# Graph kernel, aggregation stage: addresses of the accumulator computed for a group at once, and one of eight one-hot tiles made by the Vector engine

## The chip, the cores and the metric

The kernel runs on one core of one Trainium2 chip. The metric is the device time of one execution in microseconds (us). The kernel before takes 6959.23 us, the median of three runs (6958.45 to 6972.85).

## The reference

Two graph layers over 12,500 nodes with 256 features and 200,000 edges sorted by destination, each followed by a residual and a layer norm. The first layer is attention with 4 heads of 64 features:

```
scores = einsum('ehd,ehd->eh', Q[dst], K[src] + 0.2*rel[:, None, :]) / 8
w   = softmax of scores over the edges of one destination
agg = segment_sum(w[:, :, None] * V[src], dst)          # the aggregation
out = where(deg > 0, agg, V).reshape(N, 256) @ Wo + bo  # then layer norms
```

The second layer gates `leaky(x @ W2 + b2)[col]` with a sigmoid and sums it by `row`. The change touches only the aggregation of the first layer: the sum over edges of weight times value, and of the weights themselves, by destination.

## The kernel before, in words

The program runs in stages that are divided by barriers: projections and a sort, the tables of steps, the scores of the edges, the softmax's numerators, the aggregation (`aggregate`, the function of the change), the update of the nodes, the second layer (`attend`) and the last norm.

The sums live in `node_tab` in SBUF: 98 blocks of 128 nodes, each block 260 columns wide (`AW`: 256 sums of values, 4 sums of weights). The edges are cut into steps. A step is a tile of 128 edges with one block of nodes; a tile that reaches over two blocks is two steps. There are 1664 steps, taken in 416 groups of `U` = 4. The block of each step is not known when the program is built. It is read at run time from a table, `places0`, into registers of the engine.

For every group g, five engines work:

- SP starts the load of the four tiles' values from HBM into `terms` (ring of `DEEP` = 10), as soon as TensorE is through with group g - 10.
- GpSimd (POOL) multiplies the values by the weights, in place (line 1032, one instruction per group).
- ScalarE (ACT) makes the one-hot matrices. `measure(g)` takes four instructions (line 1041), one per tile: |local - iota|, where `local0` holds the edge's node within its block and `iota` the numbers 0 to 127. `encode(g)` is one instruction over the four (line 1054): relu(1 - far), which is 1 where the distance is 0. `hot` is a ring of four, and `encode(g)` waits until TensorE is through with group g - 4. `put_weights(g)` (line 1047) copies the weights beside the values.
- TensorE (PE) multiplies, per step, `hot` (128 edges by 128 nodes) with `terms` (128 edges by 260 columns) into one bank of PSUM (line 1084). An fp32 product runs as two matmuls, so there are eight per group. `ps_sum` has two buffers of four banks. TensorE waits (lines 1080 to 1083) for `hot_ready`, `weights_put`, `weighed`, and for the four additions of group g - 2.
- The Vector engine (DVE) adds each of the four results onto its block of `node_tab` (line 1072). Successive steps can have the same block, so each addition waits on the semaphore `added` until the one in front of it is complete.

The order on each engine is that of the program text. On DVE, group g is: one load of four block numbers into registers (`blocks_of`, line 150), the wait for `summed`, and then four times the wait for `added`, the computation of the address from the block number (block * 260 and so on, in the engine's registers), and the addition. The address is computed where the addition is put into the program, thus behind the wait for `added` (and, for the first of a group, behind both waits).

Of the kernel before, what the change touches and what calls it, by code (L numbers as in the profile page):

```python
# [7 lines left out]
ALU = mybir.AluOpType  # L8
ACT = mybir.ActivationFunctionType
AX = mybir.AxisListType  # L10

P = 128
# [9 lines left out]
U = 4  # L22
# [12 lines left out]
G = -(-(T + NB - 1) // TURN) * V  # L35
# [4 lines left out]
AW = D + H  # L40
# [105 lines left out]
def blocks_of(nc, eng, places, g):  # L146


    at = (g % QUARTER) * U
    return nc.values_load_multi_w_load_instructions(  # L150
        places[g // QUARTER * 32:g // QUARTER * 32 + 1, at:at + U], engines=[eng.engine], min_val=0, max_val=NB - 1,
        skip_runtime_bounds_check_because="the merged order of tiles and blocks ends at the last block")[1]
# [11 lines left out]
def gnn_kernel(nc, x, src, dst, edge_type, query, wq, bq, wk, bk, wv, bv, rel_w, wo, bo, gamma, beta,  # L164
               w1, b1, w2, b2, wa1, ba1, wa2, ba2, out):
    with ExitStack() as ctx:
# [24 lines left out]
        with ExitStack() as layer0:  # L191
            t["other0"] = layer0.enter_context(nc.sbuf_tensor("other0", [P, S], i32))
            t["places0"] = layer0.enter_context(nc.sbuf_tensor("places0", [P, S // 4], i32))
            t["score"] = layer0.enter_context(nc.sbuf_tensor("score", [P, S * H], fp32))
            t["keys"] = [layer0.enter_context(nc.sbuf_tensor(f"keys{u}", [P, F], i32)) for u in range(2)]
            t["two_signs"] = layer0.enter_context(nc.sbuf_tensor("two_signs", [P, 8], fp32))
            t["local0"] = t["keys"][0][:, 0:S].bitcast(fp32)
            project(nc, t, query, wq, bq, wk, bk, wv, bv)
            build_steps(nc, t, 0)
            edge_scores(nc, t, rel_w)  # L200
            softmax_numerators(nc, t)
            aggregate(nc, t)
# [796 lines left out]
def aggregate(nc, t):  # L999
    with ExitStack() as ctx:  # L1000
        def sb(name, shape, dt=fp32):
            return ctx.enter_context(nc.sbuf_tensor(name, shape, dt))

        def sem(name):
            return ctx.enter_context(nc.semaphore(name))

        tab = t["node_tab"]
        hot = [sb(f"a_hot{u}", [P, U, P]) for u in range(4)]
        far = [sb(f"a_far{u}", [P, U, P], bf16) for u in range(3)]
        terms = [sb(f"a_terms{u}", [P, U, AW]) for u in range(DEEP)]  # L1010
        ps_sum = [ctx.enter_context(nc.psum_tensor(f"ps_sum{u}", [P, U, 512], fp32)) for u in range(2)]
        rows_in, weights_put, weighed = [sem(f"a_rows_in{u}") for u in range(DEEP)], sem("a_weights_put"), sem("a_weighed")
        far_ready, hot_ready, summed, added = sem("a_far_ready"), sem("a_hot_ready"), sem("a_summed"), sem("a_added")
        block = ctx.enter_context(nc.Block())

        @block.sync
        def _(sp):
            for g in range(G):
                if g >= DEEP:
                    sp.wait_ge(summed, g - DEEP + 1)  # L1020
                sp.dma_start(terms[g % DEEP][:, :, 0:D],
                             t["v_edges"][g * U * P:(g + 1) * U * P, :].rearrange("(k p) d -> p k d", p=P)).then_inc(rows_in[g % DEEP], 16)

        @block.gpsimd
        def _(pool):
            for spent in t["spent"]:
                pool.sem_clear(spent)
            for g in range(G):
                pool.wait_ge(rows_in[g % DEEP], 16 * (g // DEEP + 1))
                weight = t["score"][:, g * U * H:(g + 1) * U * H].rearrange("p (k h) -> p k h", h=H)  # L1030
                by_head = terms[g % DEEP][:, :, 0:D].rearrange("p k (h d) -> p k h d", h=H)
                nc.gpsimd.tensor_tensor(by_head, by_head, weight.unsqueeze(3).broadcast_to([P, U, H, DH]), ALU.mult).then_inc(weighed, 1)  # L1032

        @block.scalar
        def _(act):
            def measure(g):
                if g >= 3:
                    act.wait_ge(hot_ready, g - 2)
                for k in range(U):
                    at = g * U + k  # L1040
                    last = nc.scalar.activation(far[g % 3][:, k, :], t["iota"][:, :], ACT.Abs, scale=-1.0, bias=t["local0"][:, at:at + 1])  # L1041
                last.then_inc(far_ready, 1)

            def put_weights(g):
                if g >= DEEP:
                    act.wait_ge(summed, g - DEEP + 1)
                nc.scalar.copy(terms[g % DEEP][:, :, D:AW],
                               t["score"][:, g * U * H:(g + 1) * U * H].rearrange("p (k h) -> p k h", h=H)).then_inc(weights_put, 1)

            def encode(g):  # L1050
                if g >= 4:
                    act.wait_ge(summed, g - 3)
                act.wait_ge(far_ready, g + 1)
                nc.scalar.activation(hot[g % 4][:, :, :], far[g % 3][:, :, :], ACT.Relu, scale=-1.0, bias=t["ones"][:, 0:1]).then_inc(hot_ready, 1)  # L1054

            measure(0)
            for g in range(G):
                if g + 1 < G:
                    measure(g + 1)
                encode(g)  # L1060
                put_weights(g)

        @block.vector
        def _(dve):
            for g in range(G):
                blocks = blocks_of(nc, dve, t["places0"], g)
                dve.wait_ge(summed, g + 1)
                for k in range(U):
                    acc = tab[:, bass.ds(blocks[k] * AW, AW)]
                    if g * U + k:  # L1070
                        dve.wait_ge(added, g * U + k)
                    dve.tensor_tensor(acc, acc, ps_sum[g % 2][:, k, 0:AW], ALU.add).then_inc(added, 1)  # L1072
            dve.wait_ge(added, G * U)

        @block.tensor
        def _(pe):
            for g in range(G):
                pe.wait_ge(hot_ready, g + 1)
                pe.wait_ge(weights_put, g + 1)
                pe.wait_ge(weighed, g + 1)  # L1080
                if g >= 2:
                    pe.wait_ge(added, (g - 1) * U)
                for k in range(U):
                    last = nc.tensor.matmul(ps_sum[g % 2][:, k, 0:AW], hot[g % 4][:, k, :], terms[g % DEEP][:, k, :],  # L1084
                                            start=True, stop=True)
                last.then_inc(summed, 1)
# [540 lines left out]
```

## Time and profile before

| | |
|---|---|
| median of three runs | 6959.23 us |
| the profiled execution's own time | 6949.19 us |
| its span, first to last instruction | 6947.4 us |
| aggregation, first to last addition starts | 3152.3 to 4136.2 us |
| mean TensorE clock over the whole span / in the aggregation | 0.77 / 1.00 |
| share of the span: PE, DVE, POOL, ACT busy | 65%, 64%, 62%, 40% |

"L1072" is line 1072 of the program. PE is TensorE's matmuls, PEld its weight loads, which run beside them. "Idle before" is the time an engine did no work ahead of the named instructions, with what it was waiting for. Instructions that an engine's sequencer handles by itself (reading a table into registers, computing an address, waiting) are not counted as busy; the profile gives them the engine's name with a q, as DVEq. Starts are in us from the start of the span.

### The profile page before, as it was taken

How to read it: one execution, taken by the hardware profiler on the slowest of the kernel's cores; microseconds unless marked ns; L12 is line 12 of the kernel's file. 1: busy time of each engine (PE TensorE's matmuls, PEld its weight loads, DVE VectorE, ACT ScalarE, POOL GpSimd, SP SyncE). 2: the span in 40 equal slices, each digit the busy share in tenths (PEclk: the TensorE clock that was granted, in tenths of full speed). 3: DMA queues.
4: the chain of work that ended last, by engine and by line, in shares of the span. 5: the costliest groups of instructions: out<-in, count | busy, mean ns of one | idle time of the engine just before them, and what ended most of it. 6: DMA issues, size and time to landing. Idle time of an engine off the chain costs nothing. (4 is left out here: it accounts for less than half of the span.)

```text
span 6947.4 us, 76698 instructions
## 1 busy us (share of the span) xinstructions
PE 4539.0 (65%) x16367; PEld 3185.0 (46%) x16367; DVE 4423.0 (64%) x9005; ACT 2772.4 (40%) x6174; POOL 4284.4 (62%) x4006
## 2 busy tenths in 40 slices
PE   9766776667667565637888879965555555555553
PEld 5555555555555444425666654433333333333331
DVE  8766776767767555576777778954444444444447
ACT  2233333333333333328888866732222222222223
POOL 0066766767767655518788755556666666666662
PEclk9867677776777677769999999976676777676766
DMA  4388998989899888826777653345555555555554
GB/s 147 118 283 292 292 294 295 294 290 298 290 299 293 292 281 275 278 66 218 223 223 222 223 160 100 103 120 140 141 143 139 141 142 139 142 142 140 142 140 133
DMA packets 920948, 1405.60 MB, mean 202 GB/s; under 512 B 92203, under 2 KB 697635, under 8 KB 920185
## 3 DMA queue, kind: packets, MB, share of 16 engines
q0 software_dynamic: 208288, 644.62, 30.0%
q1 hardware_dynamic: 645305, 640.62, 29.3%
q10 hardware_dynamic: 66914, 115.46, 5.5%
q8 instruction: 158, 2.59, 0.2%
q14 instruction: 283, 2.32, 0.1%
HBM read 1127.23 MB, written 273.11 MB: 202 GB/s over the span
## 5 line engine op out<-in xcount | busy, mean ns | idle before, releaser
L676 POOL DMA_INDIRECT s_rows<-kv_rows,other x1664 | 1749.5, 1051 | 893.4 <-issue 488.6
L1434 POOL DMA_INDIRECT t_rows<-xj_rows,other x1564 | 1492.6, 954 | 781.8 <-issue 443.1
L1526 PE MATMUL ps_xsum<-t_rows,t_att 128*128 x3328 | 1208.6, 523 | 1060.4 <-DVE t_att L1487 644.0
L1526 PEld LDWEIGHTS ps_xsum<-t_rows,t_att 128*128 128x128 f32 x3328 | 807.0, 261 | 1462.3 <-issue 1326.4
L1466 ACT ACTIVATE t_att<-t_att,t_rows 128x128 f32<-128x128 f32 x1664 | 562.4, 392 | 1689.0 <-issue 1177.4
L1487 DVE SCALAR_TENSOR_TENSOR t_att<-iota,local,t_att 128x128 f32<-128x128 f32 x1664 | 579.0, 348 | 978.8 <-ACT t_att L1466 491.7
L787 PE MATMUL ps_q<-node_tab,hot 128*128 x3328 | 1154.0, 503 | 45.0 <-issue 44.1
L785 PE MATMUL ps_rel<-rel,hot 64*128 64x64 f32 x3328 | 590.9, 332 | 853.0 <-DVE s_rows L768 587.0
L765 DVE TENSOR_TENSOR s_rows<-s_rows,ps_rel 128x1024 f32<-128x1024 f32 x416 | 506.2, 1217 | 886.8 <-remote 699.4
L785 PEld LDWEIGHTS ps_rel<-rel,hot 64*128 64x128 f32 x3328 | 531.9, 240 | 1045.1 <-issue 902.3
L692 ACT ACTIVATE hot<-apart,ones 128x1024 f32<-128x1024 bf16 x416 | 477.7, 1148 | 1241.6 <-remote 756.9
L1084 PE MATMUL ps_sum<-a_terms,a_hot 128*128 128x260 f32 x3328 | 829.8, 392 | 169.4 <-DVE node_tab L1072 155.3
L1032 POOL TENSOR_TENSOR a_terms<-a_terms,score 128x1024 f32<-128x1024 f32 x416 | 787.1, 1904 | 193.4 <-DMA a_terms<-v_edges 180.0
L787 PEld LDWEIGHTS ps_q<-node_tab,hot 128*128 128x128 f32 x3328 | 789.2, 249 | 225.6 <-issue 59.3
L1072 DVE TENSOR_TENSOR node_tab<-node_tab,ps_sum 128x260 f32 x1664 | 706.9, 425 | 289.9 <-DVE node_tab L1072 102.3
L1495 DVE TENSOR_TENSOR node_tab<-node_tab,ps_xsum 128x256 f32 x1664 | 698.0, 419 | 212.3 <-issue 166.0
L1084 PEld LDWEIGHTS ps_sum<-a_terms,a_hot 128*128 128x128 f32 x3328 | 599.1, 190 | 400.1 <-issue 326.7
L687 ACT ACTIVATE apart<-apart,minus_p 128x1024 bf16<-128x1024 bf16 x416 | 473.8, 1139 | 409.5 <-DMA apart<-what_rows 275.5
L1041 ACT ACTIVATE a_far<-iota,keys 128x128 bf16<-128x128 f32 x1664 | 530.0, 389 | 4.7 <-PEq L807 4.7
L768 DVE TENSOR_TENSOR s_rows<-s_rows,ps_q 128x1024 f32<-128x1024 f32 x416 | 507.7, 1220 | 14.3
L770 DVE TENSOR_REDUCE score<-s_rows 128x16 f32<-128x1024 f32 x416 | 507.4, 1220 | 14.2
L1054 ACT ACTIVATE a_hot<-a_far,ones 128x512 f32<-128x512 bf16 x416 | 300.3, 722 | 154.8 <-PE ps_sum L1084 154.8
(218 smaller groups left out, 3559.4 us busy)
## 6 DMA issues: line engine op xcount, KB each, us to landing
v_edges<-s_rows SPq DMA_DIRECT2D x416, 512.0 KB
a_terms<-v_edges SPq DMA_DIRECT2D x416, 512.0 KB, 4.4
apart<-what_rows SPq DMA_DIRECT2D x416, 256.0 KB
t_att<-a_rows ACTq DMA_DIRECT2D x416, 256.0 KB
s_rows<-kv_rows,other POOLq DMA_INDIRECT x1664
t_rows<-xj_rows,other POOLq DMA_INDIRECT x1564
kv_rows<-kv_out SPq DMA_DIRECT2D x97, 256.0 KB, 2.0
xj_rows<-n_hx SPq DMA_DIRECT2D x97, 130.0 KB, 2.4
```

Of the source, the lines that this page charges most:

```text
L676: pool.indirect_dma_start(out=rows[g % KV_RING][:, k, :], out_offset=None, in_=t["kv_rows"], in_offset=bass.IndirectOffsetOnAxis(ap=t["oth ...
L785: nc.tensor.matmul(ps_rel[g % 2][:, k, :], hot[g % 2][0:R, 1, k, :], rel_02[:, :], start=True, stop=True)
L787: last = nc.tensor.matmul(ps_q[g % 2][:, k, :], hot[g % 2][:, 0, k, :], t["node_tab"][:, bass.ds(blocks[k] * AW, D)], start=True, stop=True)
L1032: nc.gpsimd.tensor_tensor(by_head, by_head, weight.unsqueeze(3).broadcast_to([P, U, H, DH]), ALU.mult).then_inc(weighed, 1)
L1041: last = nc.scalar.activation(far[g % 3][:, k, :], t["iota"][:, :], ACT.Abs, scale=-1.0, bias=t["local0"][:, at:at + 1])
L1072: dve.tensor_tensor(acc, acc, ps_sum[g % 2][:, k, 0:AW], ALU.add).then_inc(added, 1)
L1084: last = nc.tensor.matmul(ps_sum[g % 2][:, k, 0:AW], hot[g % 4][:, k, :], terms[g % DEEP][:, k, :], start=True, stop=True)
L1434: pool.indirect_dma_start(out=rows[:, at:at + XW], out_offset=None, in_=t["xj_rows"], in_offset=bass.IndirectOffsetOnAxis(ap=t["other1"][: ...
L1466: last = nc.scalar.activation(att[g % ATT_RING][:, k, :], att[g % ATT_RING][:, k, :], ACT.Sigmoid, bias=rows[:, bass.ds(slot[k] * XW + D, 1)])
L1487: dve.scalar_tensor_tensor(w, t["iota"][:, :], t["local1"][:, g * U + k:g * U + k + 1], w, ALU.is_equal, ALU.mult)\
L1495: dve.tensor_tensor(acc, acc, ps_sum[g % 4][:, k, :], ALU.add).then_inc(added, 1)
L1526: nc.tensor.matmul(ps_sum[g % 4][:, k, :], att[g % ATT_RING][:, k, :], rows[:, bass.ds(slot[k] * XW, D)], start=True, stop=True)\
```

## The change

ScalarE leaves out the fourth tile's one-hot in every odd group (`by_act`). DVE makes it: `encode_last(g)` is one comparison, `iota == local`, with `iota` read from a copy of the numbers in the unused columns 384 to 511 of the last bank of `ps_sum[1]`. It writes into the same place in `hot`. It is issued behind the first addition of an odd group, for the group four later; groups 1 and 3 get theirs ahead of the loop. TensorE waits for one more semaphore, `last_hot`, in odd groups.

`sums_of(g)` reads the four block numbers and calls `lower_ap` on the four accumulators, which computes their addresses at that place in the program. It is issued between the second and the third addition of group g - 1. Ahead of the first addition, the wait for `added` now comes before that for `summed`.

```diff
+        ps_iota = ps_sum[1][:, U - 1, 512 - P:512]
+        def by_act(g):
+            return U - g % 2
...
-                for k in range(U):
+                for k in range(by_act(g)):
                     last = nc.scalar.activation(far[g % 3][:, k, :], ...)
...
-                nc.scalar.activation(hot[g % 4][:, :, :], far[g % 3][:, :, :], ACT.Relu, ...)
+                nc.scalar.activation(hot[g % 4][:, 0:by_act(g), :], far[g % 3][:, 0:by_act(g), :], ACT.Relu, ...)
...
         def _(dve):
+            def sums_of(g):
+                sums = [tab[:, bass.ds(block * AW, AW)] for block in blocks_of(nc, dve, t["places0"], g)]
+                for acc in sums:
+                    dve.lower_ap(acc)
+                return sums
+
+            def encode_last(g):
+                at = g * U + U - 1
+                if g >= 4:
+                    dve.wait_ge(summed, g - 3)
+                dve.tensor_scalar(hot[g % 4][:, U - 1, :], ps_iota, t["local0"][:, at:at + 1], None, ALU.is_equal).then_inc(last_hot, 1)
+
+            dve.tensor_copy(ps_iota, t["iota"][:, :]).then_inc(iota_put, 1)
+            dve.wait_ge(iota_put, 1)
+            encode_last(1)
+            encode_last(3)
+            sums = sums_of(0)
             for g in range(G):
-                blocks = blocks_of(nc, dve, t["places0"], g)
-                dve.wait_ge(summed, g + 1)
-                for k in range(U):
-                    acc = tab[:, bass.ds(blocks[k] * AW, AW)]
+                for k, acc in enumerate(sums):
                     if g * U + k:
                         dve.wait_ge(added, g * U + k)
+                    if k == 0:
+                        dve.wait_ge(summed, g + 1)
                     dve.tensor_tensor(acc, acc, ps_sum[g % 2][:, k, 0:AW], ALU.add).then_inc(added, 1)
+                    if k == 0 and g % 2 and g + 4 < G:
+                        encode_last(g + 4)
+                    if k == 1 and g + 1 < G:
+                        following = sums_of(g + 1)
+                sums = following
...
         def _(pe):
                 pe.wait_ge(hot_ready, g + 1)
+                if g % 2:
+                    pe.wait_ge(last_hot, max(g // 2 + 1, 2))
```

## Rows read from the trace of the kernel before

**Rows 1.** Busy time by stretch, a piece of the aggregation; (x) is instructions.

```profile
core 0: us, PE busy (x) PEld busy (x) DVE busy (x) ACT busy (x) POOL busy (x), PEclk, DMA share, GB/s
3360.00:3560.00 200.00, 168.40 (x678) 121.62 (x678) 143.51 (x338) 168.99 (x508) 160.63 (x85) 1.00 0.70 223
```

**Rows 2.** Waits, 3200 to 4100 us: total, times, longest.

```profile
POOL a_terms L1032 <- DMA a_terms<-v_edges: 176.6, 264, 1.9
PE ps_sum L1084 <- DVE node_tab L1072: 142.4, 381, 0.7
ACT a_hot L1054 <- PE ps_sum L1084: 140.9, 381, 0.7
DVE node_tab L1072 <- DVE node_tab L1072: 93.1, 398, 0.6
```

**Rows 3.** Timeline of DVE, single additions: start us, duration us; two group starts, one step.

```profile
3603.55 0.42 DVE L1072 TENSOR_TENSOR node_tab<-node_tab,ps_sum 128x260 f32 x1
3604.18 0.42 DVE L1072 TENSOR_TENSOR node_tab<-node_tab,ps_sum 128x260 f32 x1 [0.21 <-DVE node_tab L1072]
3604.75 0.42 DVE L1072 TENSOR_TENSOR node_tab<-node_tab,ps_sum 128x260 f32 x1
...
3606.52 0.43 DVE L1072 TENSOR_TENSOR node_tab<-node_tab,ps_sum 128x260 f32 x1 [0.21 <-DVE node_tab L1072]
```

**Rows 4.** Single lines: duration ns min/median/max, first and last start us.

```profile
L1072 DVEq FUSED_REGOPS  x1664: 57/57/65, 3152.2 to 4136.1; - x185
L1072 DVE TENSOR_TENSOR node_tab<-node_tab,ps_sum x1664: 424/424/427, 3152.3 to 4136.2; 128x260 f32 x185
...
L150 DVEq TENSOR_LOAD <-places x2: 340/342/344, 3603.6 to 3605.9; - x2
...
L1461 ACTq FUSED_REGOPS  x416: 13/152/1393, 4598.2 to 6849.7; - x139
...
L1080 PEldq EVENT_SEMAPHORE  x416: 51/51/51, 3148.6 to 4129.4; - x139
```

**Rows 5.** Timeline of DVE in the scores' stage: dependent instructions without addresses.

```profile
745.15 1.21 DVE L765 TENSOR_TENSOR s_rows<-s_rows,ps_rel 128x1024 f32<-128x1024 f32 x1
746.39 1.22 DVE L768 TENSOR_TENSOR s_rows<-s_rows,ps_q 128x1024 f32<-128x1024 f32 x1
747.65 1.22 DVE L770 TENSOR_REDUCE score<-s_rows 128x16 f32<-128x1024 f32 x1
```

**Rows 6.** Timeline of DVE in the second layer: addition and comparison alternate.

```profile
5500.68 0.42 DVE L1495 TENSOR_TENSOR node_tab<-node_tab,ps_xsum 128x256 f32 x1
5501.02 0.35 DVE L1487 SCALAR_TENSOR_TENSOR t_att<-iota,local,t_att 128x128 f32<-128x128 f32 x1
5501.31 0.42 DVE L1495 TENSOR_TENSOR node_tab<-node_tab,ps_xsum 128x256 f32 x1
```

**Rows 7.** Two lines of DVE with a column operand: duration ns min/median/max.

```profile
L1487 DVE SCALAR_TENSOR_TENSOR t_att<-iota,local,t_att x1664: 336/347/420, 4601.6 to 6858.5; 128x128 f32<-128x128 f32 x185
...
L545 DVE TENSOR_SCALAR hit<-ps_tile,partition x4: 1949/1950/1951, 308.9 to 4152.4; 128x1664 f32<-128x1664 f32 x4
```

**Rows 8.** Timeline of PE and ACT over one group.

```profile
3604.12 0.46 PE L1084 MATMUL ps_sum<-a_terms,a_hot 128*128 128x260 f32 x1 [0.35 <-DVE node_tab L1072]
...
3605.73 0.38 PE L1084 MATMUL ps_sum<-a_terms,a_hot 128*128 128x260 f32 x1
...
3606.15 0.72 ACT L1054 ACTIVATE a_hot<-a_far,ones 128x512 f32<-128x512 bf16 x1 [0.34 <-PE ps_sum L1084]
```

**Rows 9.** Timeline of POOL: three multiplications in a row.

```profile
3602.01 5.63 POOL L1032 TENSOR_TENSOR a_terms<-a_terms,score 128x1024 f32<-128x1024 f32 x3 [1.17 <-DMA a_terms<-v_edges]
```

More of the change, by code:

```diff
@@ L1013, in aggregate @@
         far_ready, hot_ready, summed, added = sem("a_far_ready"), sem("a_hot_ready"), sem("a_summed"), sem("a_added")
+        iota_put, last_hot = sem("a_iota_put"), sem("a_last_hot")
+        ps_iota = ps_sum[1][:, U - 1, 512 - P:512]
+        def by_act(g):
+            return U - g % 2
         block = ctx.enter_context(nc.Block())
@@ L1053, in encode @@
                 act.wait_ge(far_ready, g + 1)
-                nc.scalar.activation(hot[g % 4][:, :, :], far[g % 3][:, :, :], ACT.Relu, scale=-1.0, bias=t["ones"][:, 0:1]).then_inc(hot_ready, 1)
+                nc.scalar.activation(hot[g % 4][:, 0:by_act(g), :], far[g % 3][:, 0:by_act(g), :], ACT.Relu, scale=-1.0, bias=t["ones"][:, 0:1]).then_inc(hot_ready, 1)
             measure(0)
```

## The prediction

> **What bounds the kernel now.** I read the profile in this order: busy time by stretch, waits, the timeline of single additions, and then single lines for durations. The change touches one stage. Barriers stand on both sides of it, so whatever it gains or loses there reaches the end unchanged.
>
> In the aggregation no engine is full: of 200 us, PE is busy for 168, ACT for 169, POOL for 161 and DVE, the least, for 144, with TensorE's clock at 1.00, which is its 2.4 GHz level, and the DMA engines at 0.70 [rows 1]. The waits say who is late. PE waits for DVE's additions in nearly every group, ACT's one-hot waits for PE, and DVE waits only for itself [rows 2]. POOL waits for its loads, which come when PE frees a buffer; it runs ahead. So DVE ends last in each turn, through idle time that its busy share hides.
>
> The timeline shows this time. An addition takes 0.424 us, the next starts 0.57 after it started, and from the fourth to the next group's first it is 0.63; from group to group it is 3606.52 - 3604.18 = 2.34 us [rows 3]. Over the whole stage it is (4136.2 - 3152.3) / 415.75 = 2.366 [rows 4]; the difference, some 12 us in all, are single longer groups, and I leave it as it is. Thus 0.14 us stands between two additions. Where one DVE instruction waits for another and computes no address, only 0.03 stands there (746.39 - 745.15 - 1.21) [rows 5]. The address costs DVE about 0.11: the register instruction itself takes 0.057 [rows 4], and about 0.05 passes until what is behind it starts.
>
> **The change, part by part.** Starts of additions, from one to the next:
>
> First to second, and third to fourth: the address goes. 0.424 + 0.034 = 0.46 each, 0.11 less than now.
>
> Fourth to the next group's first: one of its two waits still stands ahead of the addition, the address doesn't. 0.63 - 0.11 = 0.53 (0.52 to 0.56).
>
> Second to third: here the sequencer reads the block numbers and computes four addresses before it can issue the third addition. The load starts as its addition does (an addition at 3603.55, the load at 3603.6) and takes 0.342 [rows 3, 4]; with about 0.025 ahead and 0.05 behind it, the addresses start at 0.42, when the addition is nearly done (0.424 + 0.034). What comes now is exposed, and no row shows it. If the four are four instructions, each 0.11 as now, the third addition starts at 0.42 + 0.43 = 0.85. If nothing of them shows, it is 0.46. The row's name says that register operations are packed, and another such row, of other content, takes 152 ns where this one takes 57 [rows 4], so one instruction can hold more than one address; the four stand side by side in the changed program, which they never do now. I take two instructions of two addresses, some 0.075 + 0.05 each: 0.42 + 0.25 = 0.67. That costs 0.10 more than now.
>
> An even group is then 0.46 + 0.67 + 0.46 + 0.53 = 2.12 us.
>
> The one-hot on DVE, in odd groups, goes between the first and second addition. Its wait is for the sum that the first addition has just used, so it is over. Its duration: a comparison of 128 columns with a column operand takes 347 ns out of SBUF, and out of PSUM 1664 columns take 1950, which is 1.04 ns a column plus 217, so 350 ns for 128 [rows 7]; both ways agree. Part of it is hidden: behind an addition that nothing makes it wait for, a comparison starts 0.34 after the addition's start, 0.08 before its end, and the next addition starts 0.29 later with an address in its way [rows 6]. Without one, 0.35 - 0.08 = 0.27: first to second is 0.61 in place of 0.46, an odd group 2.27. Bounds: 0.46 (wholly hidden) and 0.424 + 0.35 + 0.03 = 0.80 (nothing overlaps). I take 0.61, by the nearest row. What waits behind it is the second addition, and through it PE two groups on.
>
> DVE's pair of groups is 4.39 us against 2 x 2.338 = 4.68 now.
>
> What ACT is spared (one of four 0.39 us instructions and a quarter of 0.72 every second group) is worth nothing: ACT waits for PE in every group [rows 2]. POOL needs 5.63 / 3 = 1.88 a group [rows 9] and the DMA share rises to 0.70 x 2.36 / 2.2 = 0.75; both stay below. DVE's copy of the numbers, its two first one-hots and the first addresses run while POOL's first product is made: nothing.
>
> **Next in line is PE with its two buffers.** From the end of group g's last addition (3603.97) to PE's first matmul are 0.15, to the start of the last 1.61 and to its end 0.38 more, and 0.04 until ACT starts on it [rows 3, 8]: 2.18. Then come DVE's four additions of group g + 2, which take 0.46 + 0.67 + 0.46 + 0.42 = 2.01 in an even group and 2.16 in an odd one. So two groups can't go by in less than 4.19, or 4.34 by way of the odd ones. There PE has one wait more, of 0.05 [rows 4] or somewhat above: 4.40. That is level with DVE's 4.39, so the pair is 4.40. It also means that whatever goes better on DVE by 0.1 gains only a part.
>
> Sum: 208 pairs x (4.68 - 4.40) = 57 us (with 4.676: 57.4). 6949.2 - 57.4 = 6891.8 for the profiled execution. The median of the runs stands 10.0 us above that execution, so the predicted time is 6902 us.
>
> A price from a page, outside this sum: the Trainium skill, page "VectorE: DVE Perf Modes", section on the TRN2 errata, gives 120 cycles plus the columns at 0.96 GHz for PSUM to SBUF, by which I estimate the one-hot at 0.26 us. The row of 1950 ns for 1664 columns [rows 7] would be 1.86 us by it; the row disagrees, I think because of the column operand. By the page the sum would be the first rival's.
>
> **Rivals.**
>
> The one-hot costs DVE 0.09 less: first to second is 0.52 in odd groups. DVE's pair is then 4.30 and PE's way 4.31: 208 x 0.09 = 19 us more gain, 6883. Against it speaks the row of the comparison out of PSUM, which I trust (0.06).
>
> The addresses are not packed, and the load and they hold back the third addition (this ends slower). Second to third is 0.85 or, if each takes 0.12, 0.91. DVE's pair is 4.39 + 2 x (0.85 - 0.67) = 4.75, or 4.87: 15 to 40 us slower, 6974 to 6999. It decides from 0.81 upward, where 4.39 + 2 x 0.14 = 4.67 is today's pair. For it: today's addresses are one instruction each. Against: now something always stands between them (0.14, of which 0.04 for an end within 0.2%).
>
> The addresses are not kept: the addition computes its own again, and the early ones fall away. Intervals stay 0.57 and 0.63, and the one-hot adds 0.61 - 0.57 = 0.04 per pair, since it lies in the gap: 8 us, 6967. For it: in this trace no addition uses an address made ahead of another instruction. Against: an addition both reads and writes its block, and has one address row for both, so one value already serves twice (0.09).
>
> Something outside, such as a lower clock in a later stage or contention at a port by the comparisons, which eats 15 us or more of slower time: 0.03.
>
> **How the numbers follow.** The forecast holds 0.68. Its own range: second to third at 0.53 makes PE's way 4.26 and the gain 86 us, 6873; at 0.75 DVE's pair is 4.55 and the gain 26 us, 6933; thus 6870 to 6935. For 8 in 10 the range goes from 6868 to 6968, which takes in the unkept addresses and leaves out most of the unpacked ones. This kernel's time can be told from no change only beyond 0.2%, 14 us. Faster: 0.68 + 0.06 = 0.74. Within: 0.09 + 0.04 of the unpacked = 0.13. Slower: the other 0.10 of the unpacked + 0.03 = 0.13.
>
> **What would show it.** In the trace after: starts of additions 0.46, 0.67, 0.46 and 0.53 apart, with 0.61 first in odd groups; fewer address rows than 1664, each longer than 57 ns, none between a wait and its addition; a comparison of about 350 ns x208; PE still waiting for DVE, but DVE at times for PE; group to group 2.2 us. The forecast is wrong if second to third is over 0.81, if the address rows stay at 1664 with 57 ns, or if DVE now waits for PE in every group with PE's eight matmuls taking much over 2 us.

## The result, and the profile after

The changed kernel takes 6853.34 us (median of four runs, 6845.10 to 6861.07) against 6958.84 us for the kernel before, run beside it. The ratio is 0.985, 95% interval 0.9836 to 0.9864: 105 us faster. The prediction was 6902 us with a range from 6868 to 6968. The direction was right, and the gain was nearly twice what was forecast. On another chip the same pair of kernels gave 6871.64 against 6953.67 us, 0.988 (0.9862 to 0.9899).

The span went from 6947.4 to 6843.3 us, 104.1 less. The part from the first to the last addition of the aggregation took 983.9 us and takes 887.1: 96.8 less. Of the rest, 8.7 us went ahead of the stage, where the program is the same in both (the stage's first load starts at 3140.36 and at 3131.61), 0.2 came back before the first addition and 1.2 after the last. One execution differs from another by as much: the four of the changed kernel lie 16 us apart. So 97 us is what the traces show for the change. On the other chip the same part of the changed kernel took 886.8 us.

The same stretch as in [rows 1], of the changed kernel:

```profile
core 0: us, PE busy (x) PEld busy (x) DVE busy (x) ACT busy (x) POOL busy (x), PEclk, DMA share, GB/s
3360.00:3560.00 200.00, 186.97 (x752) 134.83 (x752) 167.41 (x423) 168.49 (x517) 176.98 (x94) 1.00 0.79 247
```

94 groups pass in 200 us where 85 did. ACT is as busy as before, though it has a share less to do per group, since it has more groups. The clock stayed at 1.00.

The waits, which answer to [rows 2]:

```profile
ACT a_hot L1060 <- PE ps_sum L1113: 121.3, 284, 1.0
POOL a_terms L1038 <- DMA a_terms<-v_edges: 89.2, 168, 2.5
DVE node_tab L1094 <- DVE node_tab L1094: 47.7, 192, 0.6
PE ps_sum L1113 <- DVE node_tab L1094: 43.3, 191, 0.6
DVE node_tab L1094 <- PE ps_sum L1113: 36.8, 179, 0.6
```

The last row is new in this stretch. DVE now waits for PE, and PE still waits for DVE: neither is ahead. That is the look of a loop between two engines, not of one that is full. The list leaves out idle time under 0.15 us and so counts only every second group. By starts and ends in the trace it is nearly every one: from group 10 on, PE's first matmul starts 0.15 us after the end of DVE's last addition of two groups before in all of them (0.146 to 0.148), and DVE's first addition starts 0.11 us after PE's end in 96% of them. Before the change the second time was 0.41: PE had long been done.

Single lines of DVE's program: the address rows, the one-hot, the additions (duration ns min/median/max, first and last start):

```profile
L1074 DVEq FUSED_REGOPS  x832: 93/93/104, 3132.6 to 4028.3; - x167
...
L1081 DVE TENSOR_SCALAR a_hot<-ps_sum,keys x208: 343/345/352, 3132.0 to 4021.4; 128x128 f32<-128x128 f32 x104
...
L1094 DVE TENSOR_TENSOR node_tab<-node_tab,ps_sum x1664: 412/425/427, 3143.8 to 4030.9; 128x260 f32 x185
```

832 address rows, two a group, of 93 ns each, stand in the place of 1664 of 57 ns [rows 4]. The one-hot takes 345 ns.

The timeline of DVE over an odd group, from its first addition to the next group's, with the one-hot in it, after the last two additions of the even group in front. It answers to [rows 3]:

```profile
3601.65 0.43 DVE L1094 TENSOR_TENSOR node_tab<-node_tab,ps_sum 128x260 f32 x1 [0.23 <-DVE node_tab L1094]
3602.11 0.42 DVE L1094 TENSOR_TENSOR node_tab<-node_tab,ps_sum 128x260 f32 x1
3602.74 0.42 DVE L1094 TENSOR_TENSOR node_tab<-node_tab,ps_sum 128x260 f32 x1 [0.20 <-PE ps_sum L1113]
3603.08 0.34 DVE L1081 TENSOR_SCALAR a_hot<-ps_sum,keys 128x128 f32<-128x128 f32 x1
3603.34 0.42 DVE L1094 TENSOR_TENSOR node_tab<-node_tab,ps_sum 128x260 f32 x1
3603.85 0.43 DVE L1094 TENSOR_TENSOR node_tab<-node_tab,ps_sum 128x260 f32 x1
3604.31 0.42 DVE L1094 TENSOR_TENSOR node_tab<-node_tab,ps_sum 128x260 f32 x1
3604.78 0.42 DVE L1094 TENSOR_TENSOR node_tab<-node_tab,ps_sum 128x260 f32 x1
```

First to second is 0.60, where 0.61 was forecast. Second to third is 0.51, and 0.67 was forecast. The reading of the block numbers tells why: it starts at 3603.2, ahead of the second addition, which starts at 3603.34. In the even group behind it the order is the other way round: the second addition starts at 3605.24, the reading at 3605.3:

```profile
L150 DVEq TENSOR_LOAD <-places x1: 340/340/340, 3603.2 to 3603.2; - x1
...
L150 DVEq TENSOR_LOAD <-places x1: 344/344/344, 3605.3 to 3605.3; - x1
```

```profile
3605.24 0.42 DVE L1094 TENSOR_TENSOR node_tab<-node_tab,ps_sum 128x260 f32 x1
```

Over the whole stage the reading starts 0.47 us after the group's first addition started (0.471 to 0.477), in even and in odd groups alike. The second addition starts 0.46 after the first in even groups and 0.60 in odd ones. So the reading starts 0.014 behind the second addition in the median even group, and 0.131 ahead of it in the median odd one.

The two sides of the loop. PE after DVE's last addition of the odd group, which ends at 3604.74:

```profile
3604.88 0.46 PE L1113 MATMUL ps_sum<-a_terms,a_hot 128*128 128x260 f32 x1 [0.21 <-DVE node_tab L1094]
```

And what follows PE's end of the group in front. PE's last two matmuls take from 3602.03 to 3602.63. ACT starts 0.04 after that, and DVE's addition, at 3602.74, 0.11 after it:

```profile
3602.03 0.60 PE L1113 MATMUL ps_sum<-a_terms,a_hot 128*128 128x260 f32 x2
```

```profile
3602.67 0.61 ACT L1060 ACTIVATE a_hot<-a_far,ones 128x384 f32<-128x384 bf16 x1 [0.21 <-PE ps_sum L1113]
```

### The profile page after: what moved, and what is told of

It reads as the page before. It is cut to its first block and busy times, and to the rows that moved or that the text cites. A ratio compares the mean times of both kernels' runs of the same rounds, so it can differ in the third digit from the quotient of the medians.

```text
span 6843.3 us, 75868 instructions
## 1 busy us (share of the span) xinstructions
PE 4518.4 (66%) x16367; PEld 3172.1 (46%) x16367; DVE 4457.0 (65%) x9214; ACT 2689.4 (39%) x5966; POOL 4272.2 (62%) x4006
## 5 line engine op out<-in xcount | busy, mean ns | idle before, releaser
L1038 POOL TENSOR_TENSOR a_terms<-a_terms,score 128x1024 f32<-128x1024 f32 x416 | 783.0, 1902 | 104.3 <-DMA a_terms<-v_edges 90.9
L1047 ACT ACTIVATE a_far<-iota,keys 128x128 bf16<-128x128 f32 x1456 | 469.3, 389 | 5.4 <-PEq L807 5.4
L1060 ACT ACTIVATE a_hot<-a_far,ones 128x512 f32<-128x512 bf16 (+1 forms) x416 | 278.1, 668 | 142.8 <-PE ps_sum L1113 139.3
```

## The experiments

Eleven kernels ran in three batches, each batch on one chip with the kernel before beside it. The chips differ (the kernel before took 7043.22, 6997.68 and 6953.67 us in them), so the ratios to it are what compares. The pair of groups is worked out from each trace: first to last start of an addition, divided by the 207.875 pairs between them. This mean takes in single longer groups; where a forecast left them out, the text gives the median pair beside it. The kernel before was profiled on the first chip only; the changed kernel's stage took 887.1 us there and 886.8 on another chip, so lengths of the stage can be compared across chips to some tenths of a us as far as this one pair shows.

| kernel | ratio to before (95%) | first to last addition, us | pair, us |
|---|---|---|---|
| before | 1 | 983.9 | 4.73 |
| changed | 0.985 (0.9836 to 0.9864) | 887.1 | 4.27 |
| addresses only | 0.9854 (0.9837 to 0.9870) | 882.7 | 4.25 |
| one-hot only | 1.0001 (0.9991 to 1.0011) | 986.2 | 4.74 |
| load behind fourth addition | 0.9875 (0.9858 to 0.9892) | 905.8 | 4.36 |
| release by pairs | 0.9802 (0.9785 to 0.9819) | 849.4 | 4.09 |
| loads spread, no one-hot | 0.9803 (0.9791 to 0.9816) | 842.1 | 4.05 |
| loads spread, release by pairs | 0.9723 (0.9710 to 0.9735) | 779.9 | 3.75 |
| the same with DVE's one-hot | 0.9735 (0.9722 to 0.9747) | 793.3 | 3.82 |
| waits swapped back | 0.9853 (0.9840 to 0.9865) | 879.6 | 4.23 |
| one-hot behind third | 0.9911 (0.9894 to 0.9927) | 914.6 | 4.40 |
| numbers in SBUF | 1.0042 (1.0029 to 1.0056) | 1004.8 | 4.83 |
| changed, on the last three's chip | 0.988 (0.9862 to 0.9899) | 886.8 | 4.27 |

The "last three" are the kernels one-hot behind third, numbers in SBUF, and the changed one again; they shared a chip. For the changed one 0.985 and a pair of 4.24 were expected there; its ratio is 0.988, its median pair 4.24.

### Which half did it

Addresses only:

```diff
-            return U - g % 2
+            return U
...
-            dve.tensor_copy(ps_iota, t["iota"][:, :]).then_inc(iota_put, 1)
-            dve.wait_ge(iota_put, 1)
-            encode_last(1)
-            encode_last(3)
...
-                    if k == 0 and g % 2 and g + 4 < G:
-                        encode_last(g + 4)
...
-                if g % 2:
-                    pe.wait_ge(last_hot, max(g // 2 + 1, 2))
```

> Only the addresses a group ahead; ScalarE makes all four one-hots again, DVE none. Theory A (the changed kernel's turn is set by the loop between PE and DVE over two PSUM buffers, 4.24 us a pair of groups, and the one-hot on DVE is hidden): the four additions still take 1.99 us from first start to last end, so the pair stays at 4.24, and the time at the changed kernel's, 6853 us, within 10 us; ratio to before 0.985. Theory B (taking work from ScalarE brought a part of the gain): ScalarE's one-hots come late, PE waits for them, and a good part of the 105 us is lost: 6880 us or more.

Ratio 0.9854, pair 4.25 (median 4.24): theory A, and theory B falls. The stage is 4.4 us shorter than the changed kernel's. The median pairs differ by 0.003, which is under 1 us; the rest lies in single longer groups, of which this kernel has fewer. One-hot only:

```diff
             def sums_of(g):
-                sums = [tab[:, bass.ds(block * AW, AW)] for block in blocks_of(nc, dve, t["places0"], g)]
-                for acc in sums:
-                    dve.lower_ap(acc)
-                return sums
+                return blocks_of(nc, dve, t["places0"], g)
...
-            sums = sums_of(0)
             for g in range(G):
-                for k, acc in enumerate(sums):
+                blocks = sums_of(g)
+                dve.wait_ge(summed, g + 1)
+                for k in range(U):
+                    acc = tab[:, bass.ds(blocks[k] * AW, AW)]
                     if g * U + k:
                         dve.wait_ge(added, g * U + k)
-                    if k == 0:
-                        dve.wait_ge(summed, g + 1)
...
-                    if k == 1 and g + 1 < G:
-                        following = sums_of(g + 1)
-                sums = following
```

> Only the one-hot by DVE in odd groups; block numbers and addresses as before the change, address behind the wait. Theory A: first to second addition is 0.61 in odd groups against 0.57, nothing else changes: 208 x 0.04 = 8 us slower than before, 6967 us. Theory B: 40 us or more faster than before, 6920 us or less.

Ratio 1.0001. The stage grew by 2.3 us, not 8: in odd groups first to second went from 0.569 to 0.603, as forecast, and second to third came down from 0.567 to 0.557, which was not; the median pair grew by 0.02 to 4.70. Both halves together say that the whole gain is the addresses', and the one-hot's move is worth nothing here. Theory B falls.

### What sets the time now

Release by pairs:

```diff
-                if g >= 2:
-                    pe.wait_ge(added, (g - 1) * U)
                 for k in range(U):
+                    if g >= 2 and k % 2 == 0:
+                        pe.wait_ge(added, (g - 2) * U + k + 2)
```

> The changed kernel, but PE waits for the first two additions of group g-2 before its first two products and for the other two before the rest, in place of for all four. Theory A: the loop opens by about 0.9 us, DVE's own chain of 4.05 us a pair sets the time: 208 x 0.19 = 40 us faster than the changed kernel, 6813 us, and DVE's starts are 0.46, 0.65 (0.51 in odd groups), 0.46, 0.46 apart throughout. Theory C (DVE's chain already sets it): no change, 6853 us.

Pair 4.09, and the ratio fell by 0.005, some 34 us of 6900; the stage is 37.7 us shorter. Not a single instruction of DVE was changed, and yet its turn is shorter: with four additions awaited, the loop set the time. Theory C falls. Its timeline, from an even group's third addition to the next even group's first:

```profile
3600.22 0.42 DVE L1094 TENSOR_TENSOR node_tab<-node_tab,ps_sum 128x260 f32 x1 [0.23 <-DVE node_tab L1094]
...
3601.14 0.43 DVE L1094 TENSOR_TENSOR node_tab<-node_tab,ps_sum 128x260 f32 x1
3601.48 0.35 DVE L1081 TENSOR_SCALAR a_hot<-ps_sum,keys 128x128 f32<-128x128 f32 x1
3601.74 0.41 DVE L1094 TENSOR_TENSOR node_tab<-node_tab,ps_sum 128x260 f32 x1
3602.25 0.42 DVE L1094 TENSOR_TENSOR node_tab<-node_tab,ps_sum 128x260 f32 x1
3602.71 0.42 DVE L1094 TENSOR_TENSOR node_tab<-node_tab,ps_sum 128x260 f32 x1
```

Here the odd group's first addition (3601.14) follows the fourth of the even one (0.46 after the third, at 3600.68) by 0.46 as well, where 0.53 was forecast. DVE's own pair is thus (0.46 + 0.65 + 0.46 + 0.46) + (0.60 + 0.51 + 0.46 + 0.46) = 4.06 (median 4.07): the one-hot adds nothing to it.

The load behind the fourth addition:

```diff
-                    if k == 1 and g + 1 < G:
+                    if k == U - 1 and g + 1 < G:
                         following = sums_of(g + 1)
```

> Block numbers and addresses of the next group behind the fourth addition in place of behind the second. The exposed 0.19 us moves from inside the four additions, which PE's buffer waits for, to behind them. Theory A (PE-DVE loop): four additions take 1.80 us in even groups and 1.94 in odd ones, where the one-hot isn't hidden any more; DVE's own pair is 4.19 and the loop's 4.19 by way of the odd groups: 208 x 0.05 = 10 us faster than the changed kernel, 6843 us. Theory C (DVE's own chain is what sets the changed kernel's time): DVE's pair grows by 0.14, 29 us slower, 6882 us.

This went the other way than theory A said, 18.7 us longer in the stage than the changed kernel, and not as far as C. Fourth to first took 0.72, not 0.65. The row of the wait for `summed` now stands behind the load and the addresses, so its 0.07 is exposed in every group: DVE's own pair is 2.10 + 2.23 = 4.33 (median 4.33), above the loop. PE's end stands 0.39 us ahead of the first addition in even groups and 0.26 in odd ones, so DVE does not wait for it. What the theory lacked is the price of that row; the kernel with the waits swapped back looks at it by itself. This one does not tell A from C.

### How far it goes

Loads spread, no one-hot (on the kernel with addresses only):

```diff
-                for acc in sums:
-                    dve.lower_ap(acc)
...
             sums = sums_of(0)
+            for acc in sums:
+                dve.lower_ap(acc)
...
-                    if k == 1 and g + 1 < G:
+                    if k == 0 and g + 1 < G:
                         following = sums_of(g + 1)
+                    if k in (1, 2) and g + 1 < G:
+                        for acc in following[2 * k - 2:2 * k]:
+                            dve.lower_ap(acc)
```

> Addresses only (ScalarE makes all one-hots), and DVE's register work spread: the block numbers of the next group are read behind the first addition, two addresses behind the second, two behind the third. Theory A (PE-DVE loop; each piece of register work is shorter than the addition it runs beside): DVE's starts are 0.46 apart throughout, its own pair 3.66; the four additions take 1.80 us and the loop between PE and DVE 0.15 + 1.99 + 0.11 + 1.80 = 4.04 to 4.05 a pair, against 4.24 of the changed kernel: the stage 40 us shorter than with addresses only, ratio to before 0.980. Theory D (register work is never hidden wholly, since the sequencer issues in order): the pair stays above 4.15, ratio 0.983 or more.

All additions of a group start 0.46 apart, pair 4.05, ratio 0.9803: theory A to the hundredth. Theory D falls: register work is hidden wholly in this kernel, where each piece is shorter than the addition beside it.

With the release by pairs added to that:

> As the kernel with spread loads, and PE waits for DVE's additions by pairs. Theory A: DVE's chain is 3.66 a pair, POOL's 1.86 x 2 = 3.73, ScalarE's four measures, one-hot and copy 1.90 x 2 = 3.80 to 3.9; PE's eight matmuls with two waits 1.95 x 2 = 3.9. The slowest of these sets it: a pair of 3.85 to 3.95, ratio to before 0.975. Theory D: no better than the release by pairs alone, 0.980.

Pair 3.75, the best of all, 0.9723. That is better than theory A's 3.85 to 3.95, which had ACT's pair at 3.80 to 3.9 and PE's at 3.9; theory D falls. The longest wait in its list between 3220 and 3900 us, and its busy time:

```profile
PEld ps_sum L1108 <- ACT a_hot L1060: 76.6, 280, 0.4
```

```profile
3400.00:3600.00 200.00, 199.97 (x850) 152.45 (x850) 180.22 (x425) 200.00 (x638) 200.00 (x108) 1.00 0.87 280
```

ACT, POOL and PE are busy nearly all the time, so busy time does not say which of them sets it; the waits do. What PE waits for is ACT. From group 150 on, PE's first weight load starts 0.16 us after the end of ACT's one-hot and 0.07 after that of the copy behind it in the median group, while POOL's product had been ready for 0.85 us or more in all of them. ACT's one-hots are 1.887 us apart there, which is the median pair of 3.77; the pairs before go at 3.67 to 3.74, out of one-hots that lay ready. Only here does ACT's work count. So the one-hot on DVE was tried on top (the `encode_last` lines and PE's wait put back):

> As the kernel with spread loads and release by pairs, but DVE makes the fourth one-hot in odd groups again, behind the first addition. DVE's own pair is 3.66 + 0.15 = 3.81, ScalarE's 3.4. If ScalarE set the time without it (theory B2), it is faster than without: pair 3.81 to 3.85, 10 us or more faster. If PE or POOL did (theory A2), it is the same within 4 us.

Neither: 3.82 a pair, 13.4 us longer in the stage. The intervals of the two ratios overlap, so the stage's length in the traces is what tells them apart. The load is over before the second addition has started, so no time is given back: first to second is 0.604 and second to third 0.449. The sum 3.66 + 0.15 was right, but 3.77 of ACT (the median pair without the one-hot) is less than 3.81 of DVE (the median pair with it). ACT did set the time, and DVE is a worse place for the work.

### The two steps of the forecast that were off

The one-hot behind the third addition:

```diff
-                    if k == 0 and g % 2 and g + 4 < G:
+                    if k == 2 and g % 2 and g + 4 < G:
                         encode_last(g + 4)
```

> The changed kernel with one difference: the one-hot is issued behind the third addition, not the first, so the reading of block numbers no longer lies beside it. Theory A (in the changed kernel the one-hot costs DVE nothing because the sequencer goes on to the block numbers while the one-hot still runs): first to second 0.46, second to third 0.65, third to fourth 0.60 in odd groups; the four additions then take 2.14 us there in place of 1.99, PE's loop goes from 4.24 to 4.38 a pair, 29 us slower than the changed kernel, ratio to before 0.989. Theory E (the one-hot is hidden in the gap that an addition leaves in any case): no change, 0.985.

The median pair is 4.38, as theory A has it (the mean is 4.40), and the stage is 27.8 us longer than that of the changed kernel on the same chip (914.6 against 886.8), where 29 were forecast. The ratios are 0.9911 and 0.988; their intervals just touch. Theory E falls. In an odd group second to third is 0.655 again and third to fourth 0.604: here the one-hot costs the loop its 0.15. Second, third and fourth addition of an odd group, with the one-hot behind the third:

```profile
3599.78 0.42 DVE L1094 TENSOR_TENSOR node_tab<-node_tab,ps_sum 128x260 f32 x1
3600.43 0.43 DVE L1094 TENSOR_TENSOR node_tab<-node_tab,ps_sum 128x260 f32 x1 [0.23 <-DVE node_tab L1094]
3600.77 0.35 DVE L1081 TENSOR_SCALAR a_hot<-ps_sum,keys 128x128 f32<-128x128 f32 x1
3601.03 0.42 DVE L1094 TENSOR_TENSOR node_tab<-node_tab,ps_sum 128x260 f32 x1
```

The waits swapped back:

```diff
+                    if k == 0:
+                        dve.wait_ge(summed, g + 1)
                     if g * U + k:
                         dve.wait_ge(added, g * U + k)
-                    if k == 0:
-                        dve.wait_ge(summed, g + 1)
```

> The changed kernel with one difference: ahead of a group's first addition the wait for summed comes before that for added, as before the change. Theory A: what DVE's sequencer waits for last is on the addition itself, the other is a row of its own with 0.07 behind it. DVE's own pair grows from 4.05 to 4.19 (fourth to first 0.53), and PE's loop, in which DVE now starts 0.04 and not 0.11 after PE's end, shrinks from 4.24 to 4.17. So 4.19: 10 us faster than the changed kernel, ratio to before 0.9835. Theory C (the order gave DVE 0.07 a group, and this came through): 25 us slower than the changed kernel, 0.9885.

Fourth to first is 0.529 throughout, and the median pair 4.20, as theory A has it; DVE waits for PE only twice between 3220 and 3990 us, 0.9 us in all. The stage is 7.5 us shorter than the changed kernel's (mean pair 4.23), but the ratio of times, 0.9853 (0.9840 to 0.9865), doesn't tell it from the changed kernel's 0.985, and theory A's 0.9835 lies just outside. So the pair bears theory A out and the time of the program doesn't. Theory C, 0.9885, falls.

### Why the numbers lie in PSUM

```diff
-                dve.tensor_scalar(hot[g % 4][:, U - 1, :], ps_iota, ...)
+                dve.tensor_scalar(hot[g % 4][:, U - 1, :], t["iota"][:, :], ...)
```

> The changed kernel, but the comparison reads the numbers from SBUF in place of PSUM. Theory A (the one-hot is off the loop): the pair stays 4.24 and the time within 5 us of the changed kernel's whatever the comparison takes, 0.985. Theory P (the SBUF operands disturb POOL's multiplications): POOL's 1.90 us rows get longer; time follows only if POOL passes 2.12 a group.

Both theories fall: 1.6% slower than the changed kernel on the same chip, and slower than the kernel before. POOL's median row stayed at 1902 ns (three rows of 416 took 1974 to 1990); it is DVE's that got longer:

```profile
L1081 DVE TENSOR_SCALAR a_hot<-iota,keys x208: 279/978/1997, 3148.0 to 4155.0; 128x128 f32<-128x128 f32 x104
```

The shortest takes 279 ns, less than the 345 out of PSUM, the median 978. One of them beside POOL's multiplication:

```profile
3601.84 1.90 POOL L1038 TENSOR_TENSOR a_terms<-a_terms,score 128x1024 f32<-128x1024 f32 x1 [0.86 <-DMA a_terms<-v_edges]
```

```profile
3602.97 0.86 DVE L1081 TENSOR_SCALAR a_hot<-iota,keys 128x128 f32<-128x128 f32 x1
```

The comparison starts at 3602.97, POOL's instruction ends at 3603.74, the comparison at 3603.83. It is so in the whole stage: 163 of the 208 comparisons start while POOL multiplies, and they end 0.08 us after POOL's end in the median (0.08 to 0.09 in 9 of 10). Of the 45 others, 44 take 0.28 us; the last, which starts 0.01 ahead of POOL's instruction, takes 1997 ns. So a comparison is not through before POOL is. The three longest multiplications each start 0.05 to 0.06 behind a comparison, and take 0.07 to 0.09 more than the median. The Trainium skill, page "SBUF — State Buffer", section "SBUF: two separate sides", says this: a pair of ports is shared by GpSimd and a DVE instruction in a two-port mode, whoever starts first has it for its whole instruction, and the other is blocked. These rows agree. That the comparison uses such a mode has a sign in the trace of the kernel before, where one of 1664 columns takes 1.09 us out of SBUF (line 553) and 1.95 out of PSUM [rows 7].

## Why the prediction was wrong, by its steps

**Right.** What bounded the kernel: DVE's idle time between additions, not its busy time. The price of an address, 0.11: without it additions start 0.46 apart wherever nothing else stands between them. Two packed instructions for four addresses, and second to third 0.67 in even groups (0.65 measured). The one-hot's 350 ns (345 measured) and first to second 0.61 (0.60 measured). That what ACT is spared is worth nothing, which the kernel with addresses only shows. That the loop between PE and DVE comes next, which the release by pairs shows.

**The step that failed** is the term "an odd group 2.27", and with it "2.16 in an odd one" for the four additions. It added the one-hot's 0.15 between first and second addition to a second to third of 0.67, and took the load of the block numbers to begin when the second addition begins. It begins when the sequencer has handed that addition over to the engine, 0.47 us after the first addition's start in every group. With a one-hot still running the addition waits behind it, already handed over, and the sequencer goes on to the block numbers 0.13 us before it starts. What the one-hot costs at first to second comes back at second to third: 0.51. The four additions take 0.60 + 0.51 + 0.46 + 0.42 = 1.99 in an odd group as in an even one. The one-hot behind the third addition, where no load can profit, puts the median pair at 4.38 and so shows it. The kernel with the numbers in SBUF shows it too: there the comparison takes up to 2 us, and the load still starts 0.47 us after the first addition, so second to third is 0.45 in the median odd group. The Trainium skill, page "Advanced Engine Details and Errata", section "Sequencer Loop", has this: an engine's instruction is pushed into a queue, and the sequencer reads on. This trace agrees, by the 0.13. The same list has the wait for a semaphore behind the push; that these traces do not bear out, since no load behind the second addition started before that addition's semaphore was there (0.47 us after the start of an addition that takes 0.42). In these traces the reading on waits for that semaphore.

**Two smaller terms** of the loop. PE's further wait, taken as 0.05, costs nothing: from the last addition's end at 3604.74 to PE's first matmul at 3604.88 it is 0.14 in an odd group by these rows, and 0.15 in the median of both kernels [rows 3, 8]. From PE's end to DVE's start I had 0.04; it is 0.11, since DVE's wait for `summed` became a row of its own with 0.07 until the addition. In exchange, when `summed` is there in time, the row passes beside the addition in front, and fourth to first is 0.46, not 0.53: the release by pairs has 0.46 throughout, the swapped waits 0.53. With the swapped waits PE's end stands 0.07 ahead of the first addition, so the 0.11 is gone there; that it would be 0.04 no run shows, since DVE's own pair of 4.20 sets that kernel's time. In the sum the two terms, 0.05 too much and 0.07 too little, nearly cancel, which is luck.

The loop is then 0.15 + 1.99 + 0.11 + 1.99 = 4.24 (the median pair is 4.25), where 4.40 was forecast: 0.16 x 208 = 33 us of the gain that was missing. With the failed step alone put right, DVE's own pair would have come out at 4.24 as well; but that pair is 4.06, as the release by pairs shows, so 4.24 is the loop's. The single longer groups cost some 12 us before and 6 after, and I had left them as they were: 6 us. They are regular: before, 34 additions come some 0.35 us late, 51 or 52 additions apart nearly throughout; after, 16, mostly 60 apart. What makes them late no run looks at. The forecast's 57 us is its 57.4 from 4.676; the rounded 4.68 that the sum is written with would give 58. The 57 + 33 + 6 = 96 are the 96.8 of the stage but for rounding. The 8.7 us ahead of the stage lie outside the change.

**The range.** The time fell below it, and would have done so without those 8.7 us, at 6862. Its lower end, 6868, came from the second to third addition alone. Nothing in it stood for the case that two costs I had bounded one by one, the one-hot's 0.46 to 0.80 and the load's 0.46 to 0.85, hide each other. Of the rivals, neither the unpacked addresses nor the ones computed twice came true. Nor did the cheaper one-hot: first to second is 0.60, not 0.52, and what the one-hot costs there comes back a step later.

## What to carry to other kernels

Where an engine's turns are set by short dependent instructions, look at the idle time between them and at what the sequencer does in it. An address computed behind a wait cost 0.11 us each time here, and moving it ahead of the wait gave the whole gain. Cut such work into pieces shorter than the instruction they run beside (0.46 within every group in the kernel with spread loads). Once a loop over two buffers sets the time, release the buffer in parts before moving work between engines: that gave 38 us here, and moving the one-hot gave nothing, or cost 13 us once ACT set the time. The version with spread loads and release by pairs is the best that ran, 0.9723 (0.9710 to 0.9735) of the kernel before.

## What the runs showed of the hardware

- A row of DVE's sequencer with one address took 57 ns, a row with two 93 ns.
- Of two waits ahead of an instruction on DVE, the one written last became a row of its own (that for `added` before the change, that for `summed` after it, 415 rows of 21 ns each) and the first stayed on the instruction. The row is free while something runs, and costs 0.07 us where it ends last.
- A comparison out of SBUF beside GpSimd's multiplication took up to 1997 ns instead of 279, one out of PSUM never over 352.
- DVE's sequencer read the next group's block numbers while the addition ahead of them still waited behind the one-hot, but not before that addition's semaphore was met: 0.47 us after the first addition's start, whether the one-hot took 0.28, 0.35 or 2.0 us.
